# Position matmuls of disentangled attention on two row tiles of TensorE

## What is computed

```python
q, k, v = shape_heads(hidden @ Wq + bq), shape_heads(hidden @ Wk + bk), shape_heads(hidden @ Wv + bv)
scores = einsum('bhsd,bhkd->bhsk', q, k) / sqrt(hd * 3)
pos_k, pos_q = shape_heads(re @ Wpk + bpk), shape_heads(re @ Wpq + bpq)   # re: normed table of 64 relative buckets
c2p = take_along_axis(einsum('bhsd,hkd->bhsk', q, pos_k), clip(rel + span, 0, 2 * span - 1))   # rel[s, k] = bucket(s - k)
p2c = take_along_axis(einsum('bhsd,hkd->bhsk', k, pos_q), clip(-rel + span, 0, 2 * span - 1))
scores = scores + c2p / bias_scale + p2c.swapaxes(-1, -2) / bias_scale
ctx = einsum('bhsk,bhkd->bhsd', softmax(scores), v)
x = x + (ctx @ Wo + bo)
```

## Time and profile before

| | us |
|---|---|
| median of the runs shown | 1432.5 |
| the profiled execution | 1437.29 |
| its span in the trace | 1435.5 |
| TensorE busy (matmul records / weight loads) | 1114.9 / 992.6 |
| VectorE, ScalarE, GpSimd busy | 966.4, 696.1, 553.5 |

### The profile page before, as it was taken

One profiled execution on the slowest core, in us unless ns is written; L12 is line 12 of the kernel. 1 busy time (PEld: TensorE's weight loads), 2 busy tenths in 40 slices (PEclk: granted clock), 3 DMA queues, 4 the chain that ended last, 5 costly groups with the idle time before them and its releaser, 6 DMA issues. The chain is left out here.

```text
span 1435.5 us, 31248 instructions
## 1 busy us (share of the span) xinstructions
PE 1114.9 (78%) x9281; PEld 992.6 (69%) x9281; DVE 966.4 (67%) x2968; ACT 696.1 (48%) x1448; POOL 553.5 (39%) x418
## 2 busy tenths in 40 slices
PE   4990512885626899999999999999999998730886
PEld 3980411784416889888888888888888886630786
DVE  6887731665654777777777777777777776630564
ACT  2434400443533566666666666666666664210443
POOL 0007135553002544444444444454544443026454
PEclk9995555998768999999999999999999999655999
DMA  5910042223289447464646464646565640043221
GB/s 138 206 37 0 1 178 90 76 80 92 71 289 222 103 112 165 111 163 113 164 109 165 112 162 112 162 118 156 125 148 126 147 110 1 1 159 107 63 79 50
DMA packets 75273, 165.91 MB, mean 116 GB/s; under 512 B 8249, under 2 KB 54784, under 8 KB 66528
## 3 DMA queue, kind: packets, MB, share of 16 engines
q1 hardware_dynamic: 69600, 152.75, 42.3%
q0 software_dynamic: 5632, 12.67, 2.6%
HBM read 130.76 MB, written 35.67 MB: 116 GB/s over the span
## 5 line engine op out<-in xcount | busy, mean ns | idle before, releaser
L1131 POOL TENSOR_SCALAR ds_scores<-ds_scores,ds_max 128x256 f32<-128x256 f32 x256 | 348.1, 1360 | 396.7 <-DVE ds_max L1323 396.5
L1315 DVE TENSOR_TENSOR ds_p2c<-ds_bank,ds_p2c 128x512 f32<-128x512 f32 x256 | 175.9, 687 | 95.7 <-PE ds_bank L1168 95.7
L1264 ACT ACTIVATE all_xt<-ds_bank 128x512 f32<-128x512 f32 x256 | 152.9, 597 | 150.1 <-PE ds_bank L1186 150.1
L1159 PE MATMUL ds_bank<-ds_qr,ds_tab 128*128 128x128 f32 x1536 | 190.2, 278 | 21.2 <-DVE ds_qr L1299 18.9
L1159 PE MATMUL ds_bank<-ds_kr,ds_tab 128*128 128x128 f32 x1536 | 198.8, 276 | 0.6 <-ACT ds_p2c L1248 0.6
L1159 PEld LDWEIGHTS ds_bank<-ds_qr,ds_tab 128*128 128x128 f32 x1536 | 182.0, 195 | 23.2 <-issue 23.0
L1248 ACT ACTIVATE ds_c2p_t<-ds_bank 128x512 f32<-128x512 f32 x256 | 152.7, 596 | 92.4 <-PE ds_bank L1159 91.3
L1323 DVE CUSTOM_DVE_ANT_0 ds_scores<-ds_bank,ds_p2c 128x256 f32<-128x256 f32 x512 | 195.3, 418 | 0.3 <-DVE ds_p2c L1315 0.2
L1159 PEld LDWEIGHTS ds_bank<-ds_kr,ds_tab 128*128 128x128 f32 x1536 | 185.2, 193 | 1.0 <-issue 0.8
L1248 ACT ACTIVATE ds_p2c<-ds_bank 128x512 f32<-128x512 f32 x256 | 149.3, 597 | 54.4 <-PE ds_bank L1159 54.3
L1168 PE MATMUL ds_bank<-all_constants,ds_c2p_t 128*128 128x128 f32 x1024 | 158.1, 277 | 0.0
(11 more groups left out here) (244 smaller groups left out, 1746.2 us busy)
## 6 DMA issues: line engine op xcount, KB each, us to landing
ds_qr<-scratch_qk SPq DMA_DIRECT2D x32, 1024.0 KB, 11.0
ds_kr<-scratch_qk SPq DMA_DIRECT2D x32, 1024.0 KB, 13.9
ds_tab<-scratch_tables SPq DMA_DIRECT2D x64, 248.0 KB, 10.6
slots_in<-all_zero SPq DMA_DIRECT2D x2, 5160.0 KB, 42.1
ds_qs<-scratch_q_parts SPq DMA_DIRECT2D x32, 288.0 KB
ds_ks<-scratch_k_parts SPq DMA_DIRECT2D x32, 288.0 KB
0fe_xb<-slots_in SPq DMA_DIRECT2D x40, 129.0 KB
1fe_xb<-slots_in SPq DMA_DIRECT2D x40, 129.0 KB
```

Source lines behind the costliest of these rows:

```text
L1131: pool.tensor_scalar(S[b % NS][:, 1, :], S[b % NS][:, 1, :], mx[:, 2 * b + 1:2 * b + 2], None, ALU.subtract).then_inc(s_sub1, 1)
L1159: last = pe.matmul(pb[n % 2][:, a * P:(a + 1) * P], TAB[half][:, kind, c:c + P], mov[:, :].rearrange("p (b g s) -> p g b s", b=HALF, s=16) ...
L1264: act.activation(PT[b], pt2[:, :].rearrange("p (k s) -> p k s", k=2), ACT.Exp).then_inc(s_exp, 1)
L1315: dve.tensor_tensor(z, pt1[b % 2][:, :].rearrange("p (a k) -> p a k", a=2), z, ALU.add).then_inc(s_z, 1)
```

## The change

The 128 rows are cut at partition 64: the lower half holds shifts 0 to 7, which serve the positions 8 to 15 of a group, the upper half shifts 8 to 15 and positions 0 to 7. So each position matmul becomes two, each with 64 rows, the same 128 table columns, and only the 64 moving columns whose positions it serves. The row tile 0 writes to bank 0, row tile 1 to bank 1. A near fill is now 8 groups (16 matmuls) into both banks and needs both emptied; there are 6 near fills (`RUNS`; the middle one of each kind takes its groups from both sides) and 4 far ones, which fill one bank each. ScalarE empties the two banks of a near fill with one copy each, or two of 256 columns each for the middle fills, and writes runs of 8 positions. `SHARE` becomes one fill a step for six steps and two for the last two. Loads, masks and the other steps stay.

```diff
-        FILLS = [(kind, quad, side) for kind in range(2) for quad in range(QUADS) for side in range(2)]
...
-        FILLS = near[:10] + [far[0], near[10], far[1], near[11], far[2], far[3]]
-        CONTENT_FILLS = 1 + max(n for n, f in enumerate(FILLS) if f[0] == 0)
+        RUNS = (((0, 0, 8),), ((0, 8, 4), (1, 4, 4)), ((1, 8, 8),))
+        FILLS = [("near", kind, runs) for kind in range(2) for runs in RUNS] + \
+                [("far", kind, (0, QUADS - 1)) for kind in range(2)] + [("far", kind, (1, 0)) for kind in range(2)]
+        FILLS = FILLS[:6] + [FILLS[6], FILLS[8], FILLS[7], FILLS[9]]
+        BANKS = [2 if f[0] == "near" else 1 for f in FILLS]
+        FIRST = [sum(BANKS[:n]) for n in range(len(FILLS))]
+        BM = sum(BANKS)
+        CONTENT_FILLS = FIRST[8]
...
-        SHARE = [2, 2, 2, 1, 2, 2, 2, 3]
+        SHARE = [1, 1, 1, 1, 1, 1, 2, 2]
...
-                pe.wait_ge(s_be, f + 1)
+                pe.wait_ge(s_be, f + BANKS[n])
...
-                for a in range(4):
-                    grp = 4 * quad + a
+                groups = [(side, grp) for side, grp0, count in where for grp in range(grp0, grp0 + count)]
+                for a, (side, grp) in enumerate(groups):
                     c = TABLE - SEQ + P * side - 16 * grp
-                    last = pe.matmul(pb[n % 2][:, a * P:(a + 1) * P], TAB[half][:, kind, c:c + P],
-                                     mov[:, :].rearrange("p (b g s) -> p g b s", b=HALF, s=16)[:, grp, :, :],
-                                     start=True, stop=True)
-                last.then_inc(s_bm, 1)
+                    for tile in range(2):
+                        last = pe.matmul(pb[tile][:, a * 64:(a + 1) * 64], TAB[half][tile * 64:(tile + 1) * 64, kind, c:c + P],
+                                         mov[tile * 64:(tile + 1) * 64, :].rearrange("p (b g h s) -> p g h b s", b=HALF, h=2, s=8)[:, grp, 1 - tile, :, :],
+                                         start=True, stop=True)
+                        if a == len(groups) - 1:
+                            last.then_inc(s_bm, 1)
...
+                for tile in range(2):
+                    act.wait_ge(s_bm, done + tile + 1)
+                    at = 0
+                    for side, grp, count in where:
+                        dst = to[:, side, :, :].rearrange("p b (g h s) -> p h g b s", h=2, s=8)[:, 1 - tile, grp:grp + count, :, :]
+                        last = act.activation(dst, pb[tile][:, at * 64:(at + count) * 64].rearrange("p (g b s) -> p g b s", g=count, b=HALF), ACT.Copy)
+                        at += count
+                    last.then_inc(s_be, 1)
```

More of the change, by code:

```diff
@@ L1046, in attend @@
         assert (bucket(np.arange(SEQ // 4 + 1, SEQ)) >= BUCKETS - 1).all() and (bucket(-np.arange(SEQ // 4 + 1, SEQ)) <= -BUCKETS).all()
-        FILLS = [(kind, quad, side) for kind in range(2) for quad in range(QUADS) for side in range(2)]
-        is_far = lambda quad, side: (quad, side) in ((QUADS - 1, 0), (0, 1))
-        BM = len(FILLS)
-        near, far = ([f for f in FILLS if is_far(*f[1:]) == which] for which in (False, True))
-        FILLS = near[:10] + [far[0], near[10], far[1], near[11], far[2], far[3]]
-        CONTENT_FILLS = 1 + max(n for n, f in enumerate(FILLS) if f[0] == 0)
+        RUNS = (((0, 0, 8),), ((0, 8, 4), (1, 4, 4)), ((1, 8, 8),))
[6 more added lines that the diff above has]
+        CONTENT_FILLS = FIRST[8]
         views = stacked_views(dram)
         LAG = 3
-        SHARE = [2, 2, 2, 1, 2, 2, 2, 3]
+        SHARE = [1, 1, 1, 1, 1, 1, 2, 2]
         block = stack.enter_context(nc.Block())
@@ L1140, in fill @@
             def fill(head, half, n):
-                kind, quad, side = FILLS[n]
-                f = (2 * head + half) * BM + n
+                what, kind, where = FILLS[n]
+                f = (2 * head + half) * BM + FIRST[n]
                 if n == 0:
@@ L1147, in fill @@
                 pe.wait_ge(s_masked, 2 * (2 * head + half) + kind + 1)
-                pe.wait_ge(s_be, f + 1)
+                pe.wait_ge(s_be, f + BANKS[n])
                 mov = (QR, KR)[kind][half]
-                if is_far(quad, side):
+                if what == "far":
+                    side, quad = where
                     pe.wait_ge(s_stack[half], 16 * 4 * (head + 1))
-                    pe.matmul(pb[n % 2][:, :], ENDS[half][:, kind, side * FAR:(side + 1) * FAR],
+                    pe.matmul(pb[FIRST[n] % 2][:, :], ENDS[half][:, kind, side * FAR:(side + 1) * FAR],
                               (QS, KS)[kind][half][:, :].rearrange("p (b s) -> p b s", b=HALF)[:, :, quad * 64:(quad + 1) * 64],
@@ L1228, in _ @@
             pe.sem_inc(s_av, 2)
-            for n in range(BM):
+            for n in range(len(FILLS)):
                 fill(0, 0, n)
@@ L1240, in copy @@
             def copy(head, half, n):
[L1241 to L1248, removed]
+                what, kind, where = FILLS[n]
+                done = (2 * head + half) * BM + FIRST[n]
+                to = (CT, PC)[kind][half]
+                if what == "far":
+                    side, quad = where
+                    act.wait_ge(s_bm, done + 1)
+                    act.activation(to[:, side, :, quad * 64:(quad + 1) * 64], pb[FIRST[n] % 2][:, :].rearrange("p (b s) -> p b s", b=HALF),
+                                   ACT.Copy).then_inc(s_be, 1)
+                    return
+                for tile in range(2):
[6 more added lines that the diff above has]
+                    last.then_inc(s_be, 1)
             def head_values(head, half):
```

## The result

The changed kernel takes 1494.0 us (median of four runs, 1492.6 to 1495.3), the kernel before, on the same chip, 1434.2: a ratio of 1.042, with its 95% interval 1.040 to 1.044. The profiled spans are 1490.8 and 1435.5, so 55.3 us are to be found in them.

The account below looks back on a forecast made before the run. TensorE's stream was taken to bound the attention's units. (1.77 - 0.47 + 0.36) x 31 units = +51.5, +5 for the prologue, = 56 us; 1437.3 + 56, less 4.8, gave 1489 us, range 1400 to 1530.

Parts of the forecast that it names:

- Pace of a pair: Near bursts: two row tiles load side by side, 0.112 us a pair, nothing gained (-0.5 to +0.2 us a unit).
- Change of form: Around each near burst: entering and leaving row tiles costs +0.295 us, times 6 is +1.77 us a unit.
- Wait for the last far bank: Step 7 of a unit: TensorE's wait before the last far matmul goes, -0.47 us a unit.
- Banks: Near fills: each waits until both banks are copied out, +0.36 us a unit, bounds 0 and 0.9.
- Prologue: Fills of unit 0: 16.95 us becomes about 21, +4 to +5 us, once.
- last rival: Whole kernel: the clock falls to 1.2 GHz, the unit nears 45 us, past 2000 us; chance 0.03.
- No change of form: Near bursts: row tiles need no change of form, but the bank chain binds, 1451 us; chance 0.15.
- Shorter loads: Near bursts: a tile's load is shorter or doesn't bound, 0.056 us a pair, 1340 us; chance 0.10.
- Loads in turn: Near bursts: the two row tiles load one after the other, 0.218 us a pair, 1790 us; chance 0.07.

## Why the prediction was right, and where it was not

Forecast 1489, measured 1494. The sign came out, and so did the cause within a unit, but that the sum of 56 us is close to the measured 55.3 is in part luck: the stage was priced 16 us too high and the start some 17 too low.

- *Pace of a pair, 0.112: right.* Measured 0.112, with the load as its cause (188 ns and 135 ns above). Its second half, that two row tiles load side by side, was taken from column tiles and holds.
- *Change of form, +0.295 a burst: right alone, too much in the sum.* 2.20 from the record ahead to the record behind, as worked out, and 0.29 in the run that adds one. (Inside it the first load lies bare for 0.05 and not 0.107, and the way out takes 0.20 and not 0.153, which evens out.) But where `av` stands right behind a burst (719.28 above) the engine changes from tiles to tiles, and `av`'s own way in, which was there before, is saved: some 0.15 a unit. (From the record ahead of the burst at 717.35 to the `t1` behind that `av`, at 720.28, it is 3.13, against 2.99 in the same terms before: 0.14 and not 0.295.) The step "0.295 x 6" counted both.
- *Wait for the last far bank, -0.47: too small.* The row's 12.7/27 is idle time of the matmul's engine. What the third fill in a step cost was a start 0.85 behind its predecessor instead of 0.22, that is 0.63; the run with two fills a step measured 0.65.
- *Banks, +0.36: too much.* The changed kernel's waits of TensorE's loads for copies, from 540 to 1200 us (us in total, times, longest):

```profile
PEld ds_bank L1165 <- ACT ds_c2p_t L1262: 12.0, 53, 0.3
...
PEld ds_bank L1165 <- ACT ds_p2c L1262: 4.5, 27, 0.2
```

  These are 16.5 us in 27 units, but nearly all of that lies under TensorE's own change of form. Only the fill at 714.17 comes late by it: its copies, in ScalarE's timeline, take 1.21 where the sum had 1.37.

```profile
712.90 1.21 ACT L1262 ACTIVATE ds_c2p_t<-ds_bank 128x256 f32<-128x256 f32 x4 [1.33 <-PE ds_bank L1165]
```

  The copies end at 714.11 and the fill starts at 714.17, where TensorE was ready at 712.80 + 1.25 = 714.05 (1.25 as from 716.10, the next step's t1, to the burst at 717.35): 0.12 a unit. The other fills start 3.39, 3.18 apart, which is what TensorE itself needs (3.40 and 3.18 in the prediction).
- *The unit.* 1.77 - 0.15 - 0.63 + 0.12 = +1.11, measured +1.17; the prediction had +1.66. Over the stage 35.7 us instead of 51.5. The 0.06 left are not accounted for.
- *Prologue, +4 to +5: the step that failed.* It priced the prologue at full clock, and asked only what the paired banks cost. For the banks it was about right: 6.1 in the full form. But the start cost 22.4, 14.5 of it in the prologue and 8 in the first unit. The full form with the same banks needs 47.5 from first fill to first `av`, no more than before, so nearly all of the 22.4 is the clock: bursts of 3.68 instead of 2.00, for the prologue and the first unit. The prediction had the clock in its last rival, as a matter of the whole stage; the argument against it (the experts at 1.00 with records in flight 67 of 80 us) was about full-form work, and doesn't carry over to row tiles, which left a clock that was down where it was. The windows of before that show the clock at 0.50 when the first fill starts, and again in the first unit, were not read.
- *The rivals.* "No change of form", 1451: the full form with after's order and banks took 1456, so its total was near, but the change of form exists. "Shorter loads", 1340: excluded; where the load is really halved the time is there (1337.7), but with half the product left out. "Loads in turn", 1790: not in this kernel; forced by one tile they are, at 0.226 a pair.

## What to carry to other kernels

Before a matmul is split into tiles, ask which of load and streaming sets its pace: the row tiles here shortened only the streaming, and a matmul as wide in weights as in moving columns gained nothing until the weights' columns were divided too. A wait that is hidden by another cost is worth nothing, so price two additions that fall at the same place together, and read the engine's own row of starts, not its idle share. Look at the granted clock where the changed stretch begins: a price taken at full clock doesn't hold there. And count the instructions of a loop's pass: what gains by each burst can lose everything when the pass grows (here between 1648 and 1744 of TensorE).

## What was new of the hardware

- The clock and the form of work: full-form matmuls raised the granted clock from 0.50 to 1.00 within some 6 us (before, 470 to 476); a stretch with bursts of row tiles didn't in 69 us, the last 38 of them without a gap (after, 436 to 505), but held it at 1.00 for 700 us once it was up. Two halves on one row tile left it at 0.61 on average over a millisecond. On four tiles it rose after 4 us without a gap.
- Instructions: a loop pass of 1648 TensorE instructions fetched 26 packets in the whole execution and ran without stops; one of 1744 fetched 144, with stops of up to 5.4 us, and the clock fell with them.
- Four tiles of 64x64 take 0.06 us where one full 128x128 fp32 record takes 0.112, loads included.
- A change between row tiles and the full form, out and in again, costs 0.29 us.
